# Attention and mixture-of-experts layer on one core: tokens sorted by expert pair instead of by expert

## What is computed

```
x = x + attention(layernorm(x), context)        # 16 heads of 64, causal, then Wo and bo
z = layernorm(layernorm(x), ln_g, ln_b)         # the second one with gain and bias
probs = softmax(z @ rW + rb)                    # 8 experts
the 2 largest of probs, divided by their sum, are the weights w
out_e = gelu(z @ W1[e] + b1[e]) @ W2[e] + b2[e] # 128 -> 256 -> 128
result = layernormed x + sum over the 2 chosen experts of w * out_e
```

## Time and profile before

| what | value |
|---|---|
| median of three runs | 987.0 us (986.75 to 987.83) |
| profiled execution, its own time | 988.03 us |
| span of the profiled execution | 986.3 us |
| PE busy / weight loads | 881.8 us (89%) / 744.1 us (75%) |
| DVE busy | 732.0 us (74%) |
| ACT busy | 629.3 us (64%) |
| POOL busy | 500.6 us (51%) |
| HBM read / written | 32.76 MB / 23.36 MB |

### The profile page before, as it was taken

The page is one execution under the profiler, slowest core; times in us unless marked ns, Lnnn a source line. Parts: engine busy times, 40 slices in busy tenths (PEclk is TensorE's granted clock), DMA queues, the critical chain, the costliest instruction groups (busy, mean ns, idle before and its releaser), DMA issues. The chain is left out here.

```text
span 986.3 us, 32438 instructions
## 1 busy us (share of the span) xinstructions
PE 881.8 (89%) x10928; PEld 744.1 (75%) x10928; DVE 732.0 (74%) x2217; ACT 629.3 (64%) x1352; POOL 500.6 (51%) x584
## 2 busy tenths in 40 slices
PE   6899899999999999999999999999855999999800
PEld 5688788888888887888888788888744888888700
DVE  3986778788887878888787888877755666666438
ACT  3678576686776767677676767768513556666525
POOL 3612445364644536464454646443453777777720
PEclk7999999999999999999999999999876999999955
DMA  9100101010010101101010110000013333333259
GB/s 282 38 24 2 37 11 38 5 37 22 26 32 11 37 5 37 32 17 35 8 37 5 40 32 14 24 8 18 10 33 102 111 105 106 102 107 104 74 198 331
DMA packets 55856, 56.69 MB, mean 57 GB/s; under 512 B 7383, under 2 KB 48769, under 8 KB 55809
## 3 DMA queue, kind: packets, MB, share of 16 engines
q1 hardware_dynamic: 46192, 37.01, 12.8%
q0 software_dynamic: 8704, 17.97, 5.0%
q10 hardware_dynamic: 913, 1.15, 0.3%
HBM read 32.76 MB, written 23.36 MB: 57 GB/s over the span
## 5 line engine op out<-in xcount | busy, mean ns | idle before, releaser
L735 ACT ACTIVATE pr<-pr 128x512 f32<-128x512 f32 x128 | 80.7, 631 | 192.3 <-DVE pr L1246 192.3
L856 PE MATMUL bank<-cTh,Ah 128*128 128x256 f32 x584 | 183.0, 313 | 14.9 <-DVE cTl L1232 7.9
L645 POOL DMA_INDIRECT mixed<-kf,ix_i x144 | 139.8, 971 | 56.5 <-issue 35.3
L678 ACT ACTIVATE kf<-bank 128x512 f32<-128x512 f32 x256 | 154.2, 604 | 6.2 <-PE bank L860 4.1
L860 PE MATMUL bank<-cTh,Al 128*128 128x256 f32 x512 | 146.1, 285 | 0.0
L857 PE MATMUL bank<-cTl,Ah 128*128 128x256 f32 x512 | 145.6, 284 | 0.0
L552 POOL DMA_INDIRECT slots<-zrow,slot_ix x120 | 121.5, 1013 | 34.2 <-issue 28.2
L489 POOL TENSOR_TENSOR idle_p<-half 128x1 f32<-128x1 f32 x114 | 40.4, 354 | 192.0 <-DVE slot_ix L1341 163.4
L1256 DVE TENSOR_TENSOR pr<-pr,ri 128x512 f32<-128x512 f32 x128 | 132.1, 1032 | 4.4
L856 PEld LDWEIGHTS bank<-cTh,Ah 128*128 128x128 f32 x584 | 112.7, 193 | 29.6 <-issue 17.9
L983 PE MATMUL bank<-wo_s,oT 128*128 128x128 f32 x1024 | 127.4, 278 | 2.4 <-ACT oT L731 2.4
(11 more groups left out here) (197 smaller groups left out, 1938.1 us busy)
## 6 DMA issues: line engine op xcount, KB each, us to landing
kf<-slots SPq DMA_DIRECT2D x72, 130.0 KB
xs<-in_x_dram SPq DMA_DIRECT2D x16, 256.0 KB
c_in<-in_ctx_dram SPq DMA_DIRECT2D x16, 256.0 KB, 3.0
kf<-mixed SPq DMA_DIRECT2D x8, 512.0 KB, 5.0
vf<-mixed SPq DMA_DIRECT2D x8, 512.0 KB, 5.2
out_dram<-xs SPq DMA_DIRECT2D x16, 256.0 KB, 4.3
mixed<-kf,ix_i POOLq DMA_INDIRECT x144
slots<-zrow,slot_ix POOLq DMA_INDIRECT x120, 2.4
```

The source lines that it names most:

```text
L645: pool.indirect_dma_start(out=mixed, out_offset=bass.IndirectOffsetOnAxis(ap=ix_i[buf][:, j:j + 1], axis=0), in_=y_sb[buf][:, j, :], in_of ...
L678: act.activation(kfs[par][:, 2 * u:2 * u + 2, :], ring[gr.bank(name)].rearrange("p (h t) -> p h t", h=2), ACT.Copy).then_inc(act_ev, 1)
L856: pe.matmul(ps, lh, rh, start=True, stop=False)
```

## The change

Tokens are sorted by the unordered pair of experts that they chose (28 pairs) instead of by expert. Each token's row is scattered once; the row has 259 floats: the normalised features, the residual base (x after the attention plus its normalised part, formerly kept in `xs`), the number of the token and the two weights. A slot is 256 rows of one pair (32 slots, "full") or 128 rows (28 slots, "half"), always 60 in all. Each slot applies both experts, adds the two weighted results and the residual, and scatters each row once into the DRAM table `done`, which one DRAM to DRAM DMA then copies to the output. In half slots `up` is one float32 matmul for each block. `route_b` moves from i = 2 of the group after next to the end of i = 3, in front of the sending. The W1 reload goes from the start of the kernel to the end of the attention. The padding loops run half on SP, half on ACT.

```diff
-    NT = 2 * NTOK // TILE + E
+    NPAIR = E * (E - 1) // 2
+    FULL, HALVES = NTOK // TILE, NPAIR
+    NT = FULL + HALVES
+    PAD_ROW = NPAIR * REGION
+    TOKEN, ROW = 2 * D, 2 * D + 3
-    TAB_NEXT, TAB_ALL = 1, 19
+    TAB_NEXT, TAB_ALL = 1, 50
...
# SP
-            for e in range(E):
-                row = sp.value_load(next_i[0:1, e:e + 1], min_val=0, max_val=REGION * E - TILE)
-                sp.dma_start(slots[bass.ds(row, TILE), :].rearrange("(j p) c -> p j c", p=P),
-                             pad_rows[:, :, :]).then_inc(pad_ok, 16)
+            sp.wait_ge(att_ps, NP)
+            sp.dma_start(w1_raw, W1.rearrange("e d f -> d e f")).then_inc(ld_b, 16)
             sp.wait_ge(tab, TAB_NEXT)
+            with aligned_loop(mybir.EngineType.SP, 0, NPAIR // 2) as e:
+                row = sp.value_load(next_i[0:1, bass.ds(e, 1)], min_val=0, max_val=PAD_ROW - P)
+                sp.dma_start(slots[bass.ds(row, P), :], pad_rows[:, 0, :]).then_inc(pad_ok, 16)
+            sp.wait_ge(pad_ok, 16 * (NPAIR + 1))
+            sp.wait_ge(sent, 16 * GP * NG)
+            sp.wait_ge(ent_ok, 1)
...
-            def load_y(g, buf):
-                sp.dma_start(y_in[buf], mixed[bass.ds(g * 2 * TG, 2 * TG), :].rearrange(
-                    "(p k t) d -> p k t d", p=P, k=2)).then_inc(yl[buf], 16)
...
+            sp.dma_start(out.rearrange("b s d -> b (s d)"),
+                         done[0:NTOK, :].rearrange("(b s) d -> b (s d)", s=S)).then_inc(stored, 16)
...
# POOL: one scatter for each 128 tokens instead of two
-            def send(r, rows=zrow, ix=slot_ix, upto=2 * GP):
+            def send(r, upto=GP):
                 pool.wait_ge(zn_ok, GP * r + GP)
                 if not (isinstance(r, int) and r == 0):
                     pool.wait_ge(tok_ok, r)
+                pool.wait_ge(base_ok, r + 1)
                 pool.wait_ge(ix_ok, r + 1)
+                pool.wait_ge(wt_ok, r + 1)
...
+            def add_and_send(s, k, half):
+                deep, rows = k % DEEP, 1 if is_half_slot(s, half) else TJ
+                pool.wait_ge(yv_ok, s + 1)
+                pool.tensor_tensor(y_sb[deep][:, 0:rows, :], y_sb[deep][:, 0:rows, :], zin[k][:, 0:rows, D:2 * D],
+                                   ALU.add).then_inc(ba_ok, 1)
...
+                for j in range(rows):
+                    pool.indirect_dma_start(
+                        out=done, out_offset=bass.IndirectOffsetOnAxis(ap=ix_i[deep][:, j:j + 1], axis=0),
+                        in_=y_sb[deep][:, j, :], in_offset=None).then_inc(out_s[deep], 16)
...
# PE: r_ranks has 14 matmuls of 28 columns instead of 8; experts:
+                for x in range(2):
+                    for c in range(FC):
+                        into, cols = up_bank(k, x), slice(c * P, c * P + P)
+                        if is_half_slot(s, half):
+                            last = pe.matmul(into[:, c * TILE:c * TILE + P], w_whole[deep][:, x, cols], z_whole[deep],
+                                             start=True, stop=True)
+                        else:
+                            last = split_product(into[:, c * TILE:(c + 1) * TILE], w_r[deep][:, x, cols],
+                                                 w_r[deep][:, x, HF + c * P:HF + c * P + P], z_hi[deep], z_lo[deep])
...
+                pe.matmul(into[:, :, 0:rows, :], ones_b[0:3, :],
+                          w_b[deep][:, :, :].unsqueeze(2).to_broadcast([3, 2, rows, D]), start=True, stop=False,
+                          skip_group_check=True)
+                pe.wait_ge(gl_ok, s + 1)
+                for x in range(2):
+                    for j in range(rows):
+                        for c in range(FC):
+                            last = pe.matmul(into[:, x, j, :], hid[deep][:, x, c, j * P:(j + 1) * P],
+                                             w_f[deep][:, x, c * D:(c + 1) * D], start=False, stop=(c == FC - 1),
+                                             skip_group_check=True)
...
# DVE: route_b, and where it stands
+                for twice in range(2):
+                    last = dve.tensor_tensor(weight[:, :, twice * E:twice * E + E], rt[:, 7], wide(rq[:, 7]), ALU.mult)
+                ch.step(last)
+                by = by_pair[:, :, :, :].rearrange("p k t (d e) -> p k t d e", e=E)
+                dve.tensor_tensor(by[:, 1], pair_b[:, :, :, :],
+                                  weight[:, :, 0:E].unsqueeze(2).to_broadcast([P, GP, 4, E]), ALU.mult)
+                for d in range(4):
+                    last = dve.tensor_tensor(by[:, 2, :, d, :], pair_b[:, :, d, :], weight[:, :, d + 1:d + 1 + E]
+                                             if d < 3 else weight[:, :, 4:4 + E], ALU.mult)
...
                 for k in range(2):
+                    last = dve.reduce_sum(zrow[:, :, TOKEN + 1 + k], by_pair[:, 1 + k], AX_X)
+                last.then_inc(wt_ok, 1)
...
-                    if i == 2 and not first and not second:
-                        route_b(g - 2)
...
                     normalize_half(n, par, 0)
                     normalize_half(n, par, 1)
+                    if i == 3 and not first:
+                        route_b(r)
...
+            def weights(s, k, half):
...
+                for x in range(2):
+                    e = dve.value_load(ent_i[0:1, bass.ds(s + P * (1 + x), 1)], min_val=0, max_val=E - 1)
+                    w = experts[:, bass.ds(e, 1), :].rearrange("p a c -> p (a c)")
+                    if is_half_slot(s, half):
+                        dve.tensor_tensor(w_whole[deep][:, x, :], w[:, 0:HF], w[:, HF:2 * HF], ALU.add)
+                    else:
+                        dve.tensor_copy(w_r[deep][:, x, :], w[:, 0:2 * HF])
+                    dve.tensor_copy(w_f[deep][:, x, :], w[:, 2 * HF:2 * HF + B2])
+                    last = dve.tensor_copy(w_b[deep][:, x, :],
+                                           b2_parts[:, bass.ds(e, 1), :].rearrange("p a d -> p (a d)"))
+                last.then_inc(wc_ok, 1)
...
+            def second_results(s, k, half):
...
+                for j in range(rows):
+                    last = dve.scalar_tensor_tensor(
+                        out=y_sb[deep][:, j, :], in0=down_ps(k)[:, (TJ + j) * D:(TJ + j + 1) * D],
+                        scalar=row_to[deep][:, j, 2:3], in1=y_sb[deep][:, j, :], op0=ALU.mult, op1=ALU.add)
```

More of the change, by code:

```diff
@@ new lines, in xattn_ffn_kernel @@
+        n_in, n_tok = part(NPAIR, NB_MAX), part(NPAIR)
+        n_odd, before, used, left, full_at, half_at = (part(NPAIR) for _ in range(6))
+        ends, cmp, rise = (part(NPAIR) for _ in range(3))
+        at_row = part(NPAIR + 1)
+        is_half, t_sel, t_row, ent_p, ent_s, ent_b, ent_w, ent_r = (part(1) for _ in range(8))
+        ent_cols = part(3)
+        cursor[0] = 2048
+        w1_raw = part(E, HF)
+        hid = [t.rearrange("p (x c n) -> p x c n", x=2, c=FC) for t in (
+            *(p[:, :, :].rearrange("p h s -> p (h s)") for p in pr), *(t[:, :, :].rearrange("p j q -> p (j q)") for t in (oT, pT)))]
@@ L351, in quarter, with is_half_slot, scattered, slots_of @@
             return slice(4 * (k // 2 % 2), 4 * (k // 2 % 2) + 4)
-        FIN = GP + 1
+        def is_half_slot(s, half):
+            return s >= FULL if isinstance(s, int) else half
+        def scattered(s, half, deep):
+            return 4 * TJ * (s - deep) if not is_half_slot(s, half) else (
+                16 * TJ * (FULL // DEEP) + 4 * (s - FULL - deep))
+        def slots_of(engine, turn, first, end):
+            for s in range(first, 8):
+                turn(s, s, False)
+            with aligned_loop(engine, 1, FULL // 8) as ss:
+                for k in range(8):
+                    turn(8 * ss + k, k, False)
+            for s in range(FULL, FULL + 8):
+                turn(s, s % 8, True)
+            with aligned_loop(engine, FULL // 8 + 1, NT // 8) as ss:
+                for k in range(8):
+                    turn(8 * ss + k, k, True)
+            for s in range(NT // 8 * 8, end):
+                turn(s, s % 8, True)
         def after_first(who):
@@ L637, in _ @@
[L637 to L647 removed]
+            send(NG - 1)
@@ L847, in _ @@
-            with aligned_loop(mybir.EngineType.Activation, 0, NG // 4) as gg:
-                for buf in range(4):
-                    scale_second(4 * gg + buf, buf)
+                    act.wait_ge(out_s[deep], scattered(s, half, deep))
+                for j in range(1 if is_half_slot(s, half) else TJ):
+                    last = act.activation(y_sb[deep][:, j, :], down_ps(k)[:, j * D:(j + 1) * D], ACT.Copy,
+                                          scale=row_to[deep][:, j, 1:2])
+                last.then_inc(ya_ok, 1)
@@ L852, in _, with turn @@
+            def turn(s, k, half):
+                if not isinstance(s, int) or s < NT:
+                    hi_part(s, k, half)
+                if not isinstance(s, int) or s >= 3:
+                    first_results(s - 3, (k - 3) % 8, half)
+                if not isinstance(s, int) or 1 <= s <= NT:
```

(27 more changed lines are left out.)

571 lines of the change are left out of this document (255 added, 316 removed).

## The result

The kernel after takes 1068.87 us (median of 4, 1068.14 to 1070.71) against 986.88 (4 runs, 985.28 to 987.83): ratio 1.0835, 95% interval 1.0815 to 1.0855. Slower, as forecast, by 82.0 us where I had 53, and 2 us above the upper end of the range of 1010 to 1067 us. The profiled execution took 1068.58 with a span of 1066.8.

The account below looks back on a forecast made before the run. PE was taken to bound the attention, with the tight point at the turn of a group. Terms 53 + 7 + 19 - 25.5 = +53.5 us on the median of 987.0 gave 1040 us, range 1010 to 1067.

Parts of the forecast that it names:

- term 1: Attention, turns of groups: route_b at the end of i = 3 makes cTl late and PE wait, +53 us.
- The wait, "3.3 us": Turn of a group: PE, due at 631.95, waits 3.3 us for cTl, 13 times.
- The clock, "0.7 us on average, in about half the turns": Behind a turn's wait: PE's clock drops to 0.50 in about half the turns, costing 1.4 us each, 0.7 on average.
- Rival A: Turns of groups: PE waits 2.5 to 3.3 us but the clock stays up, 1020 to 1031 us; 0.65 together with the forecast.
- "The small waits at i = 2 go": Attention at i = 2: small waits vanish, 0.3 us each, about used up by six more rank matmuls.
- Term 2: Passage from attention to experts: paddings end last, first rows reach PE later, +7 us (bounds +3 to +12).
- Term 3: Expert slots: 32 full at 3.95 us, 28 halves at 2.8 us paced by DVE, +19 us.
- Term 4: Kernel end: one 4.2 MB copy within DRAM, 15.5 us, replaces the 41.0 us final sum, -25.5 us.
- B: Expert slots: DVE paces full (4.5 us) and half (3.5 us) slots, +37 us, 1077; chance 0.10 in part or whole.
- C: Kernel end: the copy within DRAM runs at half rate, +8 us, 1048; chance 0.10.
- D: Turn of the group: DVE stays ahead, cTl comes in time, halves run at PE's 2.25 us, 972 us; chance 0.10.
- E: Sorting: scatters are halved, but rows and products rise 28%, so little is saved; counted in terms 2 and 3, no own chance.

Follow-up runs that it names:

- e2: The changed kernel with the input unit (cTl) taken ahead of statistics and mask tables at i = 0: 1054.73 us.
- e4: The changed kernel with its 14 + 14 padding DMAs written out instead of issued in two loops: 1069.26 us.
- e6: The changed kernel with route_b moved to i = 0 of the next group, behind the two shifts and the residual: 993.64 us, ratio 1.0069 to the kernel before.
- e10: e6 with the paddings issued without a loop and copied from a block in DRAM: 986.82 us, ratio 1.0005 to the kernel before.
- e3: The changed kernel with route_b moved behind the input unit of i = 0 of the next group: 1035.39 us.
- e9: The kernel before with only its old route_b moved to the end of i = 3: 1046.97 us, ratio 1.0615.

## Why the prediction was wrong, point by point

**The step that failed is term 1, the turn of a group: +53, measured +76.** The mechanism was right, in place, order and count: the weights ahead of statistics and masks on DVE, PE waiting for `cTl` (13 waits of 3.9 us and more, the first of 6.3, and a last one of 1.7), the clock at half behind it; the waits total 56.5 us. The sizes were low in two terms, and a third, put at nothing, stayed at nothing:
- *The wait, "3.3 us", is 3.95.* The weights take 2.76 us, not 2.3. The other 0.24 us lie in hand-overs between engines, which I had counted once instead of at each step: DVE starts at 407.71 where ACT's exponential is over at 407.60, PE starts 0.13 us behind `cTl`.
- *The clock, "0.7 us on average, in about half the turns", falls in all 13.* The price of one fall was about right, 1.4 forecast and 1.3 to 1.6 measured; "half the turns" was a guess from a single wait, and it was wrong. Rival A, a wait without the clock, is what ten of e2's thirteen waits of 1.7 us show, not what 3.95 us do.
- *"The small waits at i = 2 go", used up by the rank matmuls.* They went, and what used them up is that ACT's key copies come later (0.65 us where before had 0.31): nothing in sum, as forecast, but for another reason.

Together 5.3 us a group instead of 4.0, over 13 to 14 groups, 18 of the 23 us missing. The other 5 are the four groups of 49.6 us, in which the clock stayed at 0.50 twice as long, 1.3 us more each. My upper bound of +68 was too low as well: it held a turn at 5.2 us, and the twelve full groups behind the first turn are 5.7 longer on average.

**Term 2, the passage: +7, measured +15.8.** The order was right, paddings last by 9 us over the table. The size was wrong: I carried 1.06 us an issue from eight paddings to 28 on two queues, and they take 1.5 to 1.6. The change had put them into a loop on the issuing engine, which the eight of before were not, and the working left the loop out. It costs 6.3 us over the 14 issues and 2.8 us ahead of the first, as e4 shows; that is the 9 us missing. Had the loop not stood there, e4's 16.0 us would have met the "15 to 17", but the "some 3 to land" would have failed: DMA engines at a share of 1.07, 0.50 in the eight paddings before (737 to 746 us), let the rows land late. The bound of "+12", were each issue 1.2 us and more, was too low as well.

**Term 3, the slots: +19, measured +14.9.** Full slots as computed. Half slots 2.58 on average instead of 2.8, 6 us in all. As I read it, DVE's loads hide better than I had it: DVE is idle 0.24 us ahead of a weight sum on average, where I had carried 1.02 us across a load from the old tile. The tail behind PE's last product, put at 5 us, is 7.1, so 2 of the 6 are given back. The collision of POOL with DVE that the Trainium skill states (GPSIMD Engine Reference, Key points) is seen in direction but not in the size I allowed in the halves. DVE's weight sum takes 0.455 us on average and 0.405 at the shortest. POOL's addition takes 0.48 on average and 0.42 when DVE is done (the rows at 1048.43). Neither takes half as long again.

**Term 4, the end: -25.5, measured -26.2.** The copy of 4.2 MB takes 14.9 us to the end of the span, at 300 GB/s from 1052 to 1066 us as the windows count it, each byte once. The term was met in part by luck: I chose 15.5 between 13 and 24 on a rate of 390 GB/s, and no row showed such a copy.

**The rivals.** B (DVE paces both kinds of slot) and C (the copy at half rate) did not happen. D (DVE stays ahead) did not happen at the turn, where DVE's steps ran at their shortest already. But e6 shows it at another place: at i = 0 DVE finds 2.25 us in its two divisions, about what the weights step takes. D's threshold, "as long as a turn costs less than 1.1 us", took halves at PE's 2.25 us and a passage of +7: e6 has a turn that costs nothing and still loses by 0.7%, since the passage costs 16 us and its slots are those of after. E, that sorting saves little, is what is left: in e10, with both faults mended, fewer scatters and more products come out even (1.0005).

## What to carry to other kernels

Where an engine's instruction order is written by hand, ask of every moved step what stands behind it in that queue, and also what the second engine has queued behind the one it feeds: here e3 freed PE's own input and only moved the wait to ACT's queue, and e6, one position later, made the same step nearly free. When a suspected limit is taken away and the total doesn't change, read the stage in the trace before you clear it: e4 had gained 3.4 us there, and the DMA share showed a second limit behind the first. And don't carry a per-issue price from a few transfers written out to many in a loop: the loop has a price of its own, and without it the share of the DMA engines can become the next limit.

## What the hardware showed that was not expected

With the loop gone, the paddings taken from 128 partitions in pieces of 1036 bytes showed a DMA share of 1.07 at 204 GB/s (e4); the same bytes from one block of DRAM 0.74 at 226 GB/s (e10). An indirect scatter with a bound on its rows goes out 0.1 us later after what it waits for, and costs little else. PE's clock fell to 0.50 behind each of the thirteen waits of 3.9 us and more in after, behind eleven of twelve waits of 3.6 us in e9 and behind three of thirteen waits of 1.7 us in e2, at 1.3 to 1.6 us for a fall of about 3.4 us where PE was the pace. So a long wait costs more than its own length, and a short one can too. And a division on DVE that takes 0.69 us elsewhere took up to 2.22 us beside POOL's instructions, in nearly every group of the kernel before.
